# Plain float32 expert weights by DMA, and a waited memset behind every scatter: a four-layer kernel on one Trainium2 core

## The chip, the core and the metric

The kernel runs on one core of a Trainium2 chip. A core has five engines that run their own instruction streams and meet at semaphores: TensorE (PE, with its weight loads shown as PEld), VectorE (DVE), ScalarE (ACT), GpSimd (POOL) and SyncE (SP, which here only issues DMAs). Data come from HBM into SBUF by DMA; matmuls write PSUM. The metric is the device time of one execution in microseconds (us).

## What is computed

Eight sequences of 1024 tokens with 128 features go through four layers, each added to its input after a layer norm: linear attention, a mixture of experts, an RWKV-like mixing layer, and the same mixture of experts again. Cut to the part that the change touches:

```python
scores = x @ Wr.T + br                      # 8192 tokens, 8 experts
w = softmax(scores); idx = top_k(scores + biases, 2)
val = w[idx] / sum(w[idx])
h = x @ Wl1[e] + bl1[e]                     # 128 -> 2 x 256, only for the two chosen experts
y = (silu(h[:256]) * h[256:]) @ Wl2[e] + bl2[e]
out = sum over the two experts of val * y
```

## The kernel before, in words

**Stages.** Attention runs batch by batch (8 batches, each in two halves of 512 tokens) and ends each batch with the router: `choose` finds the two experts of each token, `place` ranks the tokens by expert and writes `place_i`, the queue row of each (line 1177). Then GpSimd scatters the batch's normalised tokens into `queue_dram`, sorted by expert (`scatter`, line 508): 16 indirect DMAs a batch, each of 128 rows. When all eight are queued, the first expert stage runs over 72 tiles of 256 queued tokens. The mixing layer then runs batch by batch, with router and scatter again, and the second expert stage follows.

**A tile of an expert stage.** SP loads 256 queued rows into `xtile` (lines 399 and 400). PE transposes them (955), ACT and DVE split the transposed tile into two float32r parts `xt_parts` (696, 1248). ACT copies the high part of the expert's up weights from SBUF into `tile_up` (700), DVE the low part (1253). PE makes three float32r matmuls for each of four 128-column chunks (946 to 948), ACT applies silu (690), DVE gates (1239), PE makes the down projection in float32 (965), DVE adds the bias into `ytile` (1259), and GpSimd scatters the two halves of `ytile` to `result_dram` (519). Loops hold eight tiles. The low part of all weights, `up_lo`, is made once in each expert stage by one DVE subtraction over 128 x 4096 elements (1223), in the plan that precedes the tiles.

**GpSimd's queue** sets much of the order. In attention its scatters of the batches 1 to 5 are paced: `pace` makes it wait for an event of PE between pairs of scatters. The batches 6 to 8, and all scatters of the mixing stage and of the expert stages, go back to back. In the mixing loop one turn of GpSimd's stream is `next_sums` (lines 553 and 555: four additions that make the layer's input two batches ahead), and then the 16 scatters of this batch. In `mixing`, DVE's stream has `way_in_moments` for the batch two ahead, which waits for those sums (`xsum_ready`), just before `choose` and `place`. The buffer `hffn[0]`, out of which a scatter reads, is single in the mixing layer: ACT (597) may write it for batch m only when the same half's scatters of batch m - 1 have landed (`queued`). In attention two buffers alternate.

## Time and profile before

| | us |
|---|---|
| median of three runs | 1330.14 |
| lowest, highest | 1322.95, 1336.12 |
| the profiled execution's own time | 1346.64 |
| its span, first to last instruction | 1344.8 |

| engine | busy us | share of the span |
|---|---|---|
| PE | 855.2 | 64% |
| DVE | 918.4 | 68% |
| ACT | 659.9 | 49% |
| POOL | 623.3 | 46% |

No engine is busy throughout, so the reader has to go stage by stage. Attention takes roughly the first 335 us of the span, the first expert stage 373 to 640, mixing 700 to 1000, the second expert stage 1040 to 1303. The profiled execution is 16.5 us slower than the median of the others; differences worked out on it are added to the median.

### The profile page before, as it was taken

How to read it: one execution, taken by the hardware profiler on the slowest of the kernel's cores; microseconds unless marked ns; L12 is line 12 of the kernel's file. 1: busy time of each engine (PE TensorE's matmuls, PEld its weight loads, DVE VectorE, ACT ScalarE, POOL GpSimd, SP SyncE). 2: the span in 40 equal slices, each digit the busy share in tenths (PEclk: the TensorE clock that was granted, in tenths of full speed). 3: DMA queues.
4: the chain of work that ended last, by engine and by line, in shares of the span. 5: the costliest groups of instructions: out<-in, count | busy, mean ns of one | idle time of the engine just before them, and what ended most of it. 6: DMA issues, size and time to landing. Idle time of an engine off the chain costs nothing.

```text
span 1344.8 us, 21163 instructions
## 1 busy us (share of the span) xinstructions
PE 855.2 (64%) x5110; PEld 697.5 (52%) x5111; DVE 918.4 (68%) x2976; ACT 659.9 (49%) x1788; POOL 623.3 (46%) x597
## 2 busy tenths in 40 slices
PE   3777777742178887776457667657423777887850
PEld 1665566542177887765123333323223777876750
DVE  5688888645465655555299999999953565655657
ACT  3676666611154444444576766655322444444435
POOL 3024444433545554545215555675434555555440
PEclk9788877856599888899677787787655899889885
DMA  7022222212222222221311222211092222222239
GB/s 223 16 60 79 78 79 80 65 53 68 83 75 74 68 76 69 71 58 49 110 60 63 69 83 86 94 47 38 30 254 66 71 69 75 73 70 69 62 97 315
DMA packets 144880, 111.79 MB, mean 83 GB/s; under 512 B 15779, under 2 KB 135724, under 8 KB 144464
## 3 DMA queue, kind: packets, MB, share of 16 engines
q1 hardware_dynamic: 126928, 77.58, 20.6%
q0 software_dynamic: 17920, 33.88, 7.9%
q8 instruction: 9, 0.15, 0.0%
q14 instruction: 23, 0.19, 0.0%
HBM read 62.84 MB, written 50.64 MB: 84 GB/s over the span
## 4 chain that ended last, share of the span: by engine, by line
DVE 31%; PE 31%; issue 13%; ACT 7%; another core or an unknown queue 5%; POOL 5%; DMA 4%; DVEq 2%; ACTq 1%; SPq 0%; POOLq 0%
PE banks L965 8%; PE banks L946 5%; POOL queue_dram L508 4%; PE banks L948 4%; PE banks L947 4%; DVE rope_c L1414 3%; PE banks L828 2%; PE banks L854 2%; DVE stats L1095 2%; PE banks L955 2%; ACT gated L690 1%; DVE gated L1239 1%; DMA out<-xmid 1%; DVE tile_up L1253 1%
## 5 line engine op out<-in xcount | busy, mean ns | idle before, releaser
L519 POOL DMA_INDIRECT result_dram<-ytile,result_row x288 | 283.9, 986 | 274.3 <-DVE ytile L1259 191.8
L508 POOL DMA_INDIRECT queue_dram<-hffn,place_i x192 | 222.9, 1161 | 205.8 <-DVE place_i L1177 120.6
L946 PE MATMUL banks<-xt_parts,tile_up 128*128 128x256 f32 x584 | 185.8, 318 | 87.4 <-DVE tile_up L1253 81.6
L1239 DVE SCALAR_TENSOR_TENSOR gated<-banks,tile_bias,gated 128x256 f32<-128x256 f32 x292 | 127.8, 479 | 99.9 <-ACT gated L690 76.4
L965 PE MATMUL banks<-wdown_sb,gated 128*128 x1152 | 171.2, 297 | 20.6 <-DVE gated L1239 20.5
L947 PE MATMUL banks<-xt_parts,tile_up 128*128 128x256 f32 x584 | 172.9, 296 | 0.0
L948 PE MATMUL banks<-xt_parts,tile_up 128*128 128x256 f32 x584 | 172.7, 296 | 0.0
L946 PEld LDWEIGHTS banks<-xt_parts,tile_up 128*128 128x128 f32 x584 | 119.9, 205 | 100.7 <-DVE xt_parts L1248 61.9
L965 PEld LDWEIGHTS banks<-wdown_sb,gated 128*128 128x128 f32 x1152 | 157.8, 211 | 24.3 <-issue 24.2
L690 ACT ACTIVATE gated<-banks,tile_bias 128x256 f32<-128x256 f32 x292 | 121.9, 470 | 97.4 <-PE banks L948 70.2
L696 ACT ACTIVATE xt_parts<-banks 128x256 fp32r<-128x256 f32 x150 | 57.8, 386 | 215.2 <-PE banks L955 171.7
L508 POOL DMA_INDIRECT queue_dram<-xtiles,place_i x64 | 62.3, 974 | 130.0 <-DVE place_i L1177 95.5
L947 PEld LDWEIGHTS banks<-xt_parts,tile_up 128*128 128x128 f32 x584 | 120.7, 207 | 0.0
L948 PEld LDWEIGHTS banks<-xt_parts,tile_up 128*128 128x128 f32 x584 | 120.3, 206 | 0.0
L1259 DVE TENSOR_TENSOR ytile<-banks,down_bias_sb 128x256 f32<-128x256 f32 x144 | 60.3, 419 | 86.8 <-PE banks L965 58.6
L700 ACT ACTIVATE tile_up<-up_hi 128x512 fp32r x148 | 93.3, 631 | 27.8 <-issue 27.8
L955 PE MATMUL banks<-k_sb,xtiles 128*128 128x128 f32 x300 | 62.8, 294 | 64.8 <-DMA xtiles<-queue_dram 64.8
L1248 DVE TENSOR_TENSOR xt_parts<-banks,xt_parts 128x256 fp32r<-128x256 f32 x150 | 62.8, 419 | 41.6 <-ACT xt_parts L696 33.9
L828 PE MATMUL banks<-k_sb,hmix 128*128 128x128 f32 x128 | 29.0, 370 | 86.1 <-ACT hmix L597 54.5
L955 PEld LDWEIGHTS banks<-k_sb,xtiles 128*128 128x128 f32 x300 | 41.4, 154 | 65.7 <-issue 64.0
L993 PE MATMUL banks<-hseq,wnow_sb 128*128 128x512 f32 x96 | 69.6, 815 | 6.2 <-ACT hseq L754 6.2
L828 PEld LDWEIGHTS banks<-k_sb,hmix 128*128 128x128 f32 x128 | 19.0, 185 | 98.8 <-ACT hmix L597 72.6
(210 smaller groups left out, 1986.8 us busy)
## 6 DMA issues: line engine op xcount, KB each, us to landing
xtiles<-queue_dram SPq DMA_DIRECT2D x160, 130.0 KB
qkv<-result_dram SPq DMA_DIRECT2D x24, 512.0 KB, 4.3
x_dram<-xres SPq DMA_DIRECT2D x32, 256.0 KB
result_dram<-ytile,result_row POOLq DMA_INDIRECT x288
xin<-x SPq DMA_DIRECT2D x16, 256.0 KB
xold<-x SPq DMA_DIRECT2D x16, 256.0 KB
expo<-w_up SPq DMA_DIRECT2D x2, 2048.0 KB, 9.3
xin<-x_dram SPq DMA_DIRECT2D x16, 256.0 KB
```

The source lines that it names most:

```text
L508: nc.gpsimd.indirect_dma_start(queue_dram, bass.IndirectOffsetOnAxis(ap=place_i[s][:, at:at + 1], axis=0), hffn[s][c][:, j, :], None).then ...
L519: nc.gpsimd.indirect_dma_start(result_dram, bass.IndirectOffsetOnAxis(ap=result_row[i][:, h:h + 1], axis=0), ytile[i][:, h, :], None, boun ...
L690: last = nc.scalar.activation(gated[at][:, h, :], ps_up[at][:, h, :], ACT.Silu, bias=tile_bias[(i + 1) % STEP][:, h:h + 1])
L700: nc.scalar.activation(tile_up[i % 2][:, 0, :], up_hi[:, bass.ds(e * (2 * HID), 2 * HID)].bitcast(F32), ACT.Copy).then_inc(whi_ready, 1)
L828: last = nc.tensor.transpose(dst[:, j * P:(j + 1) * P], src[:, j, 0:D], ident)
L946: nc.tensor.matmul(ps_up[at][:, h, :], hi, xt_parts[at][:, 0, :], start=True, stop=False)
L947: nc.tensor.matmul(ps_up[at][:, h, :], hi, xt_parts[at][:, 1, :], start=False, stop=False)
L948: last = nc.tensor.matmul(ps_up[at][:, h, :], lo, xt_parts[at][:, 0, :], start=False, stop=True)
L955: last = nc.tensor.transpose(ps_xt[(i + 3) % 2][:, part * P:(part + 1) * P], xtile[slot][:, part, 0:D], ident)
L965: last = nc.tensor.matmul(y, gated[i % 2][:, h, tokens], wdown_sb[:, bass.ds(e * (HCH * D) + h * D, D)], start=(h == 0), stop=(h == HCH - 1))
L993: nc.tensor.matmul(part, wnow_sb[:, i, :], hseq[:, 1 + c * CHUNK:1 + (c + 1) * CHUNK], start=True, stop=False)
L1239: last = nc.vector.scalar_tensor_tensor(gated[at][:, h, :], ps_up[at][:, HCH + h, :], tile_bias[(i + 1) % STEP][:, HCH + h:HCH + h + 1], g ...
```

## The change

Two things are changed at once.

**The expert stages.** The up projection is done in plain float32, with four matmuls a tile in place of twelve. The split of the tile (DVE 1248) and both weight copies (ACT 700, DVE 1253) go; ACT issues a 256 KB DMA a tile that brings the expert's up weights from HBM into one of four slots. ACT empties the transposed tile with one copy. `up_hi`, `up_lo` and their making (POOL 539, DVE 1223) go. Loops hold 12 tiles, `xtile` and `ytile` have 6 slots instead of 8, `gated` has 3 instead of 2, and PE works two tiles ahead of the down projection.

**The scatters.** Behind each of the 256 scatters to `queue_dram` and the 288 to `result_dram`, GpSimd clears a 128 x 16 buffer, waits for that memset's own semaphore, and clears the semaphore. The pacing by PE's events goes. `hffn` has two buffers of its own rather than sharing `xtiles`.

```diff
-STEP = 8
+STEP = 12
+SLOTS = 6
+WSLOTS = 4
+GSLOTS = 3
+SPACER = 16
@@ GpSimd
+            def space():
+                nc.gpsimd.memset(spacer[:], 0.0).then_inc(spaced, 1)
+                pool.wait_ge(spaced, 1)
+                pool.sem_clear(spaced)
...
-            def scatter(m, s, paced):
+            def scatter(m, s):
...
-                        if paced and c + j:
-                            pace(m, c * TPC + j)
-                            pool.sem_inc(place_taken, 1)
                         for k in range(TOPK):
...
                                 hffn[s][c][:, j, :], None).then_inc(queued[s][c], 16)
+                            space()
...
+                                ytile[i % SLOTS][:, h, :], None, bounds_check=NO_RESULT - 1, oob_is_err=False).then_inc(y_stored[i % SLOTS], 16)
+                            space()
...
-            pool.wait_ge(experts_in, 16 * len(EXPERTS))
-            nc.gpsimd.tensor_copy(up_hi[:], up_raw).then_inc(hi_ready, 1)
@@ ACT
-                    nc.scalar.activation(xt_parts[(i + 3) % 2][:, 0, :], ps_xt[(i + 3) % 2], ACT.Copy).then_inc(xhi_ready, 1)
+                    nc.scalar.activation(xt[i % 2][:], ps_xt[i % 2], ACT.Copy).then_inc(xt_ready, 1)
...
-                    nc.scalar.activation(tile_up[i % 2][:, 0, :], up_hi[:, bass.ds(e * (2 * HID), 2 * HID)].bitcast(F32), ACT.Copy).then_inc(whi_ready, 1)
+                    nc.scalar.dma_start(tile_up[i % WSLOTS][:], w_up[:, bass.ds(e * (2 * HID), 2 * HID)]).then_inc(tile_up_in[i % WSLOTS], 16)
@@ PE
-                        nc.tensor.matmul(ps_up[at][:, h, :], hi, xt_parts[at][:, 0, :], start=True, stop=False)
-                        nc.tensor.matmul(ps_up[at][:, h, :], hi, xt_parts[at][:, 1, :], start=False, stop=False)
-                        last = nc.tensor.matmul(ps_up[at][:, h, :], lo, xt_parts[at][:, 0, :], start=False, stop=True)
+                        last = nc.tensor.matmul(ps_up[i % 2][:, h, :], tile_up[i % WSLOTS][:, h * P:(h + 1) * P], xt[i % 2][:],
+                                                start=True, stop=True)
@@ DVE
-                nc.vector.tensor_tensor(up_lo[:], up_raw, up_hi[:].bitcast(F32), ALU.subtract).then_inc(lo_ready, 1)
...
-                    nc.vector.tensor_tensor(xt_parts[at][:, 1, :], ps_xt[at], xt_parts[at][:, 0, :].bitcast(F32),
-                                            ALU.subtract).then_inc(xlo_ready, 1)
...
-                    nc.vector.tensor_copy(tile_up[i % 2][:, 1, :], up_lo[:, bass.ds(e * (2 * HID), 2 * HID)].bitcast(F32)).then_inc(wlo_ready, 1)
```

On GpSimd, at the start of an expert stage, the stores of the first two tiles and a half stood like this before (519 is the scatter of one half of `ytile`, the register row belongs to the loop):

```order
L514 UNCONDITIONAL_BRANCH
L514 ISA
L519 DMA result_dram<-ytile,result_row 16520x128 [waits ytile_ready]
L519 DMA result_dram<-ytile,result_row 16520x128
L516 REGISTER_ALU
L519 DMA result_dram<-ytile,result_row 16520x128 [waits ytile_ready]
L519 DMA result_dram<-ytile,result_row 16520x128
```

The same place of the changed kernel (515 is now that scatter, 491 the memset, 493 the clear of its semaphore, which carries the wait):

```order
L515 DMA result_dram<-ytile,result_row 16518x128 [waits ytile_ready]
L491 MEMSET spacer 128x16
L493 ISA [waits spaced]
L515 DMA result_dram<-ytile,result_row 16518x128
L491 MEMSET spacer 128x16
L493 ISA [waits spaced]
L512 REGISTER_ALU
L515 DMA result_dram<-ytile,result_row 16518x128 [waits ytile_ready]
```

Between any two scatters there now stand a memset and a wait for it. The scatters to `queue_dram` (503 now) have the same three rows each.

On DVE, one tile of the expert loop before:

```order
L1231 SCALAR_TENSOR_TENSOR result_row<-xtiles,expert_all 128x2
L1253 ISA
L1253 COPY tile_up<-up_lo 128x512
L1239 SCALAR_TENSOR_TENSOR gated<-banks,tile_bias,gated 128x256 [waits silu_ready]
L1239 SCALAR_TENSOR_TENSOR gated<-banks,tile_bias,gated 128x256
L1259 ISA [waits y_stored1,y_ready]
L1259 TENSOR_TENSOR ytile<-banks,down_bias_sb 128x256
L1245 ISA
L1245 COPY tile_bias<-up_bias_sb 128x4
L1246 REGISTER_ALU
L1248 TENSOR_TENSOR xt_parts<-banks,xt_parts 128x256 [waits xhi_ready]
```

and one tile of it now (1243 gates, 1251 adds the bias, 1232 makes the result rows, 1237 takes the bias columns):

```order
L1243 SCALAR_TENSOR_TENSOR gated<-banks,tile_bias,gated 128x256 [waits silu_ready]
L1243 SCALAR_TENSOR_TENSOR gated<-banks,tile_bias,gated 128x256
L1249 REGISTER_ALU
L1251 ISA [waits y_stored1,y_ready]
L1251 TENSOR_TENSOR ytile<-banks,down_bias_sb 128x256
L1232 ISA [waits y_stored4,xtile_in4]
L1232 SCALAR_TENSOR_TENSOR result_row<-xtile,expert_all 128x2
L1237 ISA
L1237 COPY tile_bias<-up_bias_sb 128x4
```

The weight copy and the split are gone, and the bias addition stands directly behind the gate of the tile two ahead.

## Rows read from the trace of the kernel before

**Rows 1.** The page's head: the profiled span.

```profile
span 1344.8 us, 21163 instructions
```

**Rows 2.** Timeline, expert stage: start us, us, engine, line, operation [idle before <-releaser].

```profile
401.05 0.42 DVE L1259 TENSOR_TENSOR ytile<-banks,down_bias_sb 128x256 f32<-128x256 f32 x1 [1.63 <-remote]
...
402.35 0.98 POOL L519 DMA_INDIRECT result_dram<-ytile,result_row  x1 [2.31 <-DVE ytile L1259]
...
403.97 1.06 PE L965 MATMUL banks<-wdown_sb,gated 128*128 x8
...
404.87 0.38 PE L955 MATMUL banks<-k_sb,xtiles 128*128 128x128 f32 x2
...
408.18 0.38 ACT L696 ACTIVATE xt_parts<-banks 128x256 fp32r<-128x256 f32 x1 [2.98 <-PE banks L955]
```

**Rows 3.** Scatters to results: duration ns min/median/max, first and last start us.

```profile
L519 POOL DMA_INDIRECT result_dram<-ytile,result_row x288: 980/983/1182, 373.5 to 1301.8; - x144
```

**Rows 4.** Timeline, POOL: last result scatter of stage one, first of two.

```profile
637.27 0.98 POOL L519 DMA_INDIRECT result_dram<-ytile,result_row  x1 [0.30 <-issue]
...
1040.05 1.00 POOL L519 DMA_INDIRECT result_dram<-ytile,result_row  x1 [15.57 <-DVE ytile L1259]
```

**Rows 5.** Windows, one mixing batch: busy us (x) of PE, PEld, DVE, ACT, POOL; PEclk, DMA, GB/s.

```profile
755.47:796.13 40.66, 27.82 (x85) 15.15 (x85) 38.93 (x100) 25.88 (x53) 24.88 (x20) 0.75 0.25 78
```

**Rows 6.** Timeline of that mixing batch, POOL and DVE.

```profile
756.30 2.66 POOL L508 DMA_INDIRECT queue_dram<-hffn,place_i  x1 [11.04 <-DVE place_i L1177]
...
779.44 0.96 POOL L508 DMA_INDIRECT queue_dram<-hffn,place_i  x1 [0.30 <-issue]
780.43 1.27 POOL L553 TENSOR_TENSOR xold<-xin,qkv 128x512 f32<-128x512 f32 x1
...
784.34 1.60 POOL L555 TENSOR_TENSOR xold<-xold,qkv 128x512 f32<-128x512 f32 x1
...
787.87 1.65 DVE L1095 BATCH_NORM_STATS2 stats<-xold 128x6 f32<-128x128 f32 x8 [0.19 <-DVE rotated L1380]
...
795.96 0.17 DVE L1177 CAST place_i<-place_f 128x16 int32<-128x16 f32 x1
...
796.95 2.67 POOL L508 DMA_INDIRECT queue_dram<-hffn,place_i  x1 [11.01 <-DVE place_i L1177]
```

**Rows 7.** Timeline, POOL: a memset at the kernel's start.

```profile
0.22 0.10 POOL L1572 MEMSET const-float32-0.0<- 128x1 f32 x1 [0.22 <-issue]
```

**Rows 8.** Timeline: last scatter of batch 15 of 16, and who waits for it.

```profile
980.13 0.96 POOL L508 DMA_INDIRECT queue_dram<-hffn,place_i  x1 [0.30 <-issue]
...
986.19 0.17 DVE L1146 COPY hffn<-k_sb 128x4 f32<-128x4 f32 x1 [5.12 <-DMA queue_dram<-hffn,place_i]
```

**Rows 9.** Timeline, POOL: first scatters of the attention batches 5, 6 and 7.

```profile
223.66 0.96 POOL L508 DMA_INDIRECT queue_dram<-xtiles,place_i  x1 [7.62 <-DVE place_i L1177]
...
257.64 0.96 POOL L508 DMA_INDIRECT queue_dram<-hffn,place_i  x1 [7.64 <-DVE place_i L1177]
...
297.64 0.96 POOL L508 DMA_INDIRECT queue_dram<-xtiles,place_i  x1 [19.93 <-DVE place_i L1177]
```

**Rows 10.** Timeline, POOL: first, eighth and last scatter of batch 16.

```profile
998.30 0.95 POOL L508 DMA_INDIRECT queue_dram<-hffn,place_i  x1 [17.21 <-DVE place_i L1177]
...
1009.20 5.19 POOL L508 DMA_INDIRECT queue_dram<-hffn,place_i  x1 [0.31 <-issue]
...
1023.52 0.96 POOL L508 DMA_INDIRECT queue_dram<-hffn,place_i  x1 [0.31 <-issue]
```

**Rows 11.** DVE's work on `up_lo`: duration ns min/median/max, first and last start us.

```profile
L1253 DVE CAST tile_up<-up_lo x148: 414/421/657, 364.4 to 1297.6; 128x512 fp32r x148
L1223 DVE TENSOR_TENSOR up_lo<-expo,up_hi x2: 4418/4418/4419, 343.0 to 1009.1; 128x4096 fp32r<-128x4096 f32 x2
```

**Rows 12.** Timeline, PE: one float32 matmul with 512 columns, as two instructions.

```profile
794.92 1.02 PE L994 MATMUL banks<-hseq,wpast_sb 128*128 128x512 f32 x2
```

**Rows 13.** DMA issues: count, KB, median us to landing.

```profile
expo<-w_up SPq DMA_DIRECT2D x2, 2048.0 KB, 9.3
```

More of the change, by code:

```diff
@@ L144, in program @@
             rotated = [rotated0, rotated1]
[L145 removed]
+        tile_up = [sb(f"tile_up{i}", [P, 2 * HID]) for i in range(WSLOTS)]
         rope2 = sb("rope2", [P, TPC, 2 * D])
@@ L321, in program @@
         FIRST, SECOND = 0, 1
-        N_TURN, N_WEIGHTS, N_UP, N_GATE, N_BACK = (XTILES + ahead for ahead in (3, 2, 1, 1, 0))
         PLACE_STEPS = 3
@@ new lines, in weights, with steps @@
+                def weights(i, e):
+                    nc.scalar.dma_start(tile_up[i % WSLOTS][:], w_up[:, bass.ds(e * (2 * HID), 2 * HID)]).then_inc(tile_up_in[i % WSLOTS], 16)
+                def steps(n, left):
+                    first = n * STEP
+                    e = read(mybir.EngineType.Activation, tile_expert[0:1, bass.ds(first + 2 + WSLOTS, min(STEP, left - 2 - WSLOTS))], NE - 1)
+                    for i in range(STEP):
+                        if i + 2 < left:
+                            silu_up(first + i + 2, i + 2)
+                        if i + 2 + WSLOTS < left:
+                            weights(i + 2 + WSLOTS, e[i])
+                        if i + 4 < left:
+                            empty_x(first + i + 4, i + 4)
@@ new lines, in experts @@
+                act.wait_ge(table_ready, f + 1)
+                e = read(mybir.EngineType.Activation, tile_expert[0:1, 0:2 + WSLOTS], NE - 1)
+                for t in range(WSLOTS):
+                    weights(t, e[t])
+                empty_x(0, 0)
+                empty_x(1, 1)
+                for t in range(2):
+                    silu_up(t, t)
+                    weights(t + WSLOTS, e[t + WSLOTS])
+                    empty_x(t + 2, t + 2)
+                with act.Fori(0, LAST) as n:
+                    steps(n, 2 * STEP)
@@ L720, in weigh @@
+                steps(LAST, STEP)
             def weigh(y, g, done, first=0, step=1):
@@ L964, in down, with steps @@
                         for h in range(HCH):
-                            last = nc.tensor.matmul(y, gated[i % 2][:, h, tokens], wdown_sb[:, bass.ds(e * (HCH * D) + h * D, D)],
+                            last = nc.tensor.matmul(y, gated[i % GSLOTS][:, h, tokens], wdown_sb[:, bass.ds(e * (HCH * D) + h * D, D)],
                                                     start=(h == 0), stop=(h == HCH - 1))
                     last.then_inc(y_ready, 1)
-                pe.wait_ge(table_ready, f + 1)
-                for t in range(-3, 0):
-                    if t + 1 >= 0:
-                        up(t, t)
-                    turn_x(t, t)
-                with pe.Fori(0, XTILES // STEP) as n:
-                    first = n * STEP
-                    e = read(mybir.EngineType.PE, tile_expert[0:1, bass.ds(first, STEP)], NE - 1)
-                    for i in range(STEP):
-                        up(first + i, i)
-                        down(first + i, i, e[i])
-                        turn_x(first + i, i)
+                def steps(n, left):
+                    e = read(mybir.EngineType.PE, tile_expert[0:1, bass.ds(n * STEP, STEP)], NE - 1)
+                    for i in range(STEP):
+                        if i + 2 < left:
+                            up(n, i + 2)
+                        if i + 4 < left:
+                            turn_x(n, i + 4)
+                        down(n, i, e[i])
+                pe.wait_ge(table_ready, f + 1)
+                turn_x(0, 0)
+                turn_x(0, 1)
+                for t in range(2):
+                    up(0, t)
+                    turn_x(0, t + 2)
+                with pe.Fori(0, LAST) as n:
+                    steps(n, 2 * STEP)
+                steps(LAST, STEP)
             def turn_in(m):
@@ new lines, in steps @@
+                def steps(n, left):
+                    e = read(mybir.EngineType.DVE, tile_expert[0:1, bass.ds(n * STEP, min(STEP + 4, left))], NE - 1)
+                    for i in range(STEP):
+                        if i + 2 < left:
+                            gate(n, i + 2)
+                        add_bias(n, i, e[i])
+                        if i + 3 < left:
+                            place_rows(n, i + 3)
+                        if i + 4 < left:
+                            take_bias(i + 4, e[i + 4])
@@ L1282, in invert_norms @@
+                dve.wait_ge(table_ready, f + 1)
+                e = read(mybir.EngineType.DVE, tile_expert[0:1, 0:4], NE - 1)
+                for t in range(4):
+                    take_bias(t, e[t])
+                for t in range(3):
+                    place_rows(0, t)
+                for t in range(2):
+                    gate(0, t)
+                with dve.Fori(0, LAST) as n:
+                    steps(n, 2 * STEP)
+                steps(LAST, STEP)
             def invert_norms(m):
```

221 lines of the change are left out of this document (81 added, 140 removed).

## The prediction, made before the changed kernel ran

> **What bounds the kernel now.** I read the windows by stage first, then the timeline of one expert tile and of one mixing batch, because the shares of the whole span say nothing (no engine is over 70%).
>
> In the expert stages GpSimd makes 144 result scatters each. The first starts at 373.5 and the last at 637.27, and in the second stage they run from 1040.05 to 1301.8 [rows 3, 4]: 143 steps of 1.845 and of 1.83 us, or 3.69 us a tile. A scatter takes 0.98 us, and one without a wait before it starts 0.30 after the last, a step of 1.28 [rows 4], so GpSimd alone would need 2.6 us a tile. It idles because its input is late, and the timeline shows why: PE's transposes of a tile are shown as done at 405.25, and ACT, which waits for nothing else, copies them at 408.18, 2.9 us late [rows 2], while scatters run back to back. So PE's messages get through late during bursts of scatters, and this costs the stage about 1 us a tile. I take that as the thing that a pause behind each scatter can cure.
>
> In mixing a batch takes 40.66 us, and DVE is busy for 38.93 of them [rows 5]. But GpSimd is nearly as tight. Its chain: 16 scatters from 756.30, the last starting at 779.44; sums from 780.43 to 785.94; DVE takes the sums at 787.87 and ends `place` at 796.13; the next scatter starts at 796.95 [rows 6]. The sums are ready only 1.93 us before DVE wants them. This is a closed loop (scatters, sums, moments, place, scatters) with 1.93 us of slack in 40.65.
>
> **The price of a paused scatter.** This is the term on which all rests. A scatter that follows a wait starts late: `ytile` is ready at 401.47 and the scatter starts at 402.35, 0.88 later [rows 2]; `place_i` is ready at 796.13 and the scatter starts at 796.95, 0.82 later [rows 6]. Without a wait the gap is 0.30 [rows 4], since the next scatter is made ready while the last runs. The new wait takes that overlap away. Between the end of a scatter and the next start there then are: 0.03 to the memset (a POOL addition starts 0.03 after a scatter's end [rows 6]), 0.10 for the memset [rows 7] (1 column there, 16 here; I take 0.11), 0.05 for the clear (no POOL row; between nothing and the wait's own 0.1), and 0.82 or 0.88. For `queue_dram` a step becomes 0.96 + 0.03 + 0.11 + 0.05 + 0.82 = **1.97 us** against 1.26; for the results 0.98 + 0.03 + 0.11 + 0.05 + 0.88 = **2.05**, I use 2.04. Bounds: the cheapest is that the wait costs only the memset, 1.26 + 0.14 = 1.40; the dearest that DVE keeps the memsets waiting too, 2.2.
>
> **Expert stages.** Is another engine over the 2 x 2.04 = 4.08 us that GpSimd now needs for a tile? PE: a float32 matmul of 512 columns is two instructions that end within 1.02 us, so 0.43 each once they follow one another (1.02 less the last one's 0.59), thus 0.21 for 256 columns; eight of them make 1.7 for up. Down takes 0.9 (eight instructions from 403.97 to the transposes at 404.87) and the transposes 0.25 [rows 2, 12]. That is 2.85 a tile, less than 4.08. DVE loses a weight copy of 0.42 [rows 11] and the split, ACT a copy, and none of this lies on GpSimd's path any more. The weight DMA carries 256 KB; 2048 KB landed in 9.3 us [rows 13], so one lands between 1.2 and 9.3, and it is issued four tiles, 16 us, ahead: hidden. ACT's issue of it is hidden by ACT's idle time, since only one copy and two activations a tile are left to it. With six slots GpSimd finds finished tiles waiting, so what PE and DVE save is not seen. Each stage: 143 x (2.04 - 1.845) = **+27.9**, and 143 x (2.04 - 1.83) = **+30.0**. The cure of PE's late messages is real and is worth nothing here, because the new bound is above the old.
>
> **Mixing.** The 16 scatters spanned 23.14 us between first and last start, where 15 x 1.26 = 18.9: 4.2 us are lost to DVE (one scatter took 2.66 [rows 6]). I keep the 4.2. New: 15 x 1.97 + 4.2 = 33.7 to the last start, 1.2 to its end, memset and sums' start, 5.5 of sums (780.43 to 785.94), 0.1, then 8.26 of DVE from the moments to `place` (787.87 to 796.13), and 0.82: 49.6 against 40.65, +8.9 a batch. This holds for the five intervals inside the loop: +45. For the last two batches the sums are not in the way but the buffer is: in batch 15 the last scatter starts at 980.13 and DVE and ACT may write at 986.19, 6.1 later; the next scatter starts at 998.30, 12.1 after that [rows 8, 10]. With a landing of 4 us (6.1 in a burst is the upper bound) the interval is 33.7 + 4 + 12.1 = 49.8 against 41.3 now: +8 each, +16. Together **+61**.
>
> **Scatters that nothing hides.** After batch 16 all wait for its scatters: 998.30 to 1023.52, 25.22 us [rows 10]. Of these 4.2 are the scatter at 1009.20, held for 5.19 us while DVE makes `up_lo` for 4.42 [rows 10, 11]; that goes. New: 15 x 1.97 + 2.05 of other stalls = 31.6, **+6.4**. After batch 8 it is the same, +6.4. Against it stands attention: batch 6 takes 33.98 from batch 5 (paced), batch 7 takes 40.0 behind unpaced scatters [rows 9]; the pause gives back these 6.0. GpSimd needs 0.8 + 16 x 1.97 = 32.3 us a batch, just under the 33.98, so attention is not stretched. Net **+0.4**.
>
> Here a rule of the Trainium skill bears on the sum. The rows show that DVE's 148 weight copies of 0.42 us leave the result scatters alone, at 980, 983 and at most 1182 ns [rows 3, 11], while the subtraction into `up_lo` holds a scatter for 5.19 us [rows 10]. The page "SBUF — State Buffer", section "SBUF: two separate sides", says that a DVE copy in float32 within SBUF locks GpSimd out of its port, so that it can't write descriptors. By that rule the change would also free up to 148 x 0.42 = 62 us by dropping the copies (an estimate by that page); by the row it frees only the subtraction. The row decides.
>
> **Sum.** 27.9 + 30.0 + 61 + 6.4 + 0.4 = 125.7. The span of 1344.8 [rows 1] becomes 1471, the profiled execution's 1346.6 becomes 1472, and the median of 1330.1 becomes 1456. I say 1455.
>
> **Rivals.**
> (1) *The pause is cheap, and the expert stages run at PE's pace* (ends on the other side). If a pause costs only the memset, steps are 1.40, GpSimd needs 2.8 a tile and PE's 2.85 decides, some 3.1 with the granted clock below full now and then. A stage of 72 tiles is 223 us against 264, twice -41; mixing +3; attention -6; the bare scatters -4. About 1240. For: late messages of PE are in the trace. Against: 0.82 and 0.88 stand before every scatter with a wait. It decides below a step of about 1.68: the sum falls by 4.2 us for each 0.01 of the step (286 steps in the experts, 105 in mixing, 30 bare).
> (2) *Mixing is not stretched.* DVE at 38.93 of 40.66 looks like the bound, and if sums or buffers have slack that I don't see, the 61 fall away: 1395. Against: 1.93 us between sums and moments.
> (3) *The pause is dearer.* If DVE's long operations hold memsets as they hold scatters, a step is 2.2: +0.2 x 421 = +84, so 1540. To this belongs the clock: mixing is granted 0.75 [rows 5]; with PE idle for a third of each tile, the expert stages may fall to the lower of its two levels. At 0.75 a tile is 2.85 / 0.75 = 3.8, still under 4.08; at the lower level throughout it is 5.7, +117 a stage. The Trainium skill, page "TensorE: Matmul & The Clock Gate", section "HAM oscillation — how this bites in real kernels", says that idle gaps of PE bring the clock down; by it this would come true wherever PE waits for GpSimd, but a PE at half clock would be busy again, so I give it little.
>
> **How the numbers follow.** Forecast (1400 to 1505): 0.63. Rival 1: 0.12. Rival 2: 0.12. Rival 3: 0.13. The range reaches down to rival 2 and up to where the step is 2.15, and leaves out rival 1 and the end of rival 3: 1380 to 1530. About 1% is what a measurement can tell from no change. Faster by over 1% is rival 1, 0.12; within 1% needs the step between 1.65 and 1.71, 0.02; slower 0.86.
>
> **What would show it.** Right: result scatters about 2.04 apart without idle time by `ytile`, windows of a mixing batch near 49.6, ACT's copy of a transposed tile directly after PE. Wrong: GpSimd idle for `ytile` in the expert stages (then PE or ACT's DMA issue is the bound), steps of 1.4 to 1.7 between scatters, or DVE without a wait for the sums in mixing.

## The result, and the profile after

The changed kernel takes 1488.40 us (median of four, 1485.62 to 1491.13) against 1333.13 for the kernel before on the same chip (median of four, 1322.95 to 1338.26): 1.1175 times as long, 95% interval 1.1102 to 1.1249. Slower, as forecast, and inside the range of 1380 to 1530, 33 us above the predicted 1455. The profiled execution took 1485.62 us; its span is 1483.4 against 1344.8 [rows 1], so +138.6 on the spans where the sum said +125.7. Of all the executions reported below one, of `e4_late_wait`, ran at a mean granted clock of 0.67 (0.77 to 0.81 in the others) and took 1331.54 us; it is left out of the figures of that kernel.

The page of the changed kernel, its head and the groups that carry the change (the columns are: count | busy us, mean ns of one | idle us of the engine before them, and what ended most of it):

```profile
span 1483.4 us, 20450 instructions
...
PE 893.9 (60%) x4498; PEld 695.6 (47%) x4499; DVE 780.1 (53%) x2662; ACT 574.5 (39%) x1630; POOL 691.4 (47%) x1138
...
L503 POOL DMA_INDIRECT queue_dram<-hffn,place_i x256 | 290.1, 1133 | 368.2 <-POOL spacer L491 171.3
L515 POOL DMA_INDIRECT result_dram<-ytile,result_row x288 | 282.8, 982 | 314.7 <-POOL spacer L491 135.4
...
L491 POOL MEMSET spacer<- 128x16 f32 x544 | 75.8, 139 | 0.3
```

The scatters last as long as before (982 ns, [rows 3]), yet GpSimd now idles 683 us before them (368.2 and 314.7), and the largest single part of each is put down to its own clear (171.3 and 135.4). The shares of PE, DVE and ACT fell (64, 68 and 49% before). The timeline of POOL in the expert stage shows one pause after the other:

```profile
450.77 0.98 POOL L515 DMA_INDIRECT result_dram<-ytile,result_row  x1 [0.86 <-issue]
451.74 0.14 POOL L491 MEMSET spacer<- 128x16 f32 x1
452.90 0.98 POOL L515 DMA_INDIRECT result_dram<-ytile,result_row  x1 [1.02 <-POOL spacer L491]
453.86 0.14 POOL L491 MEMSET spacer<- 128x16 f32 x1
454.87 0.98 POOL L515 DMA_INDIRECT result_dram<-ytile,result_row  x1 [0.86 <-issue]
```

From one scatter to the next it is 2.13 and 1.97 us in turn, where rows 4 show 1.28 without a wait. The clear itself takes 0.14; the 0.86 and 1.02 behind it are GpSimd with nothing to do until its next scatter begins. The longer one stands ahead of a tile's first scatter, behind the wait for `ytile`, the loop's sum and a semaphore count.

The waits of the first expert stage, 375 to 668 us (engine, line, what it waited for: us in total, times, longest):

```profile
DVE result_row L1232 <- DMA result_dram<-ytile,result_row: 163.7, 63, 5.1
...
POOL result_dram L515 <- issue: 67.3, 68, 3.4
POOL result_dram L515 <- POOL spacer L491: 63.9, 66, 1.0
...
POOL result_dram L515 <- DVE ytile L1251: 7.1, 7, 1.0
```

GpSimd waits for a finished tile 7 times, 7.1 us in all, and each of these waits is as long as the 1.02 us that stand there anyway. VectorE stands 163.7 us until a scatter out of the slot that it wants has landed, and ACT and TensorE wait behind VectorE.

And one mixing batch, its window from one end of `place` to the next (columns as in rows 5), with POOL's and VectorE's places in it:

```profile
845.17:894.50 49.33, 28.00 (x87) 14.67 (x85) 36.23 (x100) 26.44 (x53) 27.03 (x36) 0.72 0.21 64
```

```profile
846.00 2.65 POOL L503 DMA_INDIRECT queue_dram<-hffn,place_i  x1 [9.19 <-DVE place_i L1184]
...
878.98 0.96 POOL L503 DMA_INDIRECT queue_dram<-hffn,place_i  x1 [0.80 <-POOL spacer L491]
...
880.97 1.25 POOL L544 TENSOR_TENSOR xold<-xin,qkv 128x512 f32<-128x512 f32 x1 [0.89 <-POOL spacer L491]
...
884.87 1.26 POOL L546 TENSOR_TENSOR xold<-xold,qkv 128x512 f32<-128x512 f32 x1
...
886.24 1.65 DVE L1102 BATCH_NORM_STATS2 stats<-xold 128x6 f32<-128x128 f32 x8 [11.98 <-POOL xold L546]
...
894.32 0.17 DVE L1184 CAST place_i<-place_f 128x16 int32<-128x16 f32 x1
...
895.32 2.65 POOL L503 DMA_INDIRECT queue_dram<-hffn,place_i  x1 [9.18 <-DVE place_i L1184]
```

VectorE, busy for 38.93 of 40.66 us before [rows 5], now stands some 12 us in each batch (11.98 in this one) waiting for GpSimd's sums. It no longer bounds the batch.

Stage by stage, from the starts of scatters and the ends of `place`:

| stretch | before | after | difference | forecast |
|---|---|---|---|---|
| start to `place` of batch 1 | 89.7 | 89.0 | -0.7 | |
| to `place` of batch 8 | 241.8 | 220.3 | -21.4 | |
| to the last scatter of batch 8 | 25.9 | 42.7 | +16.7 | these three +0.4 |
| to the first result scatter | 16.2 | 18.6 | +2.4 | 0 |
| first to last result scatter | 263.8 | 298.6 | +34.9 | +27.9 |
| to `place` of batch 9 | 77.4 | 77.3 | 0.0 | 0 |
| to `place` of batch 14 | 203.5 | 247.6 | +44.1 | +45 |
| to `place` of batch 16 | 79.3 | 97.6 | +18.3 | +16 |
| to the last scatter of batch 16 | 26.1 | 32.0 | +6.0 | +6.4 |
| to the first result scatter | 16.5 | 18.8 | +2.2 | 0 |
| first to last result scatter | 261.7 | 298.0 | +36.3 | +30.0 |
| to the end | 43.0 | 42.9 | -0.1 | 0 |

### The profile page after: what moved, and what is told of

It reads as the page before. It is cut to its first block, busy times and chain, and to the rows that moved or that the text cites. A ratio compares the mean times of both kernels' runs of the same rounds, so it can differ in the third digit from the quotient of the medians.

```text
span 1483.4 us, 20450 instructions
## 1 busy us (share of the span) xinstructions
PE 893.9 (60%) x4498; PEld 695.6 (47%) x4499; DVE 780.1 (53%) x2662; ACT 574.5 (39%) x1630; POOL 691.4 (47%) x1138
## 4 chain that ended last, share of the span: by engine, by line
POOL 42%; issue 32%; DVE 8%; DMA 6%; PE 6%; ACT 3%; POOLq 2%; DVEq 1%; SPq 0%; ACTq 0%
POOL queue_dram L503 19%; POOL result_dram L515 16%; POOL spacer L491 6%; DMA result_dram<-ytile,result_row 2%; PE banks L854 1%; DMA out<-xmid 1%; PE banks L945 1%; POOL xold L544 1%; POOLq L493 1%; DVE stats L1102 1%; DMA queue_dram<-hffn,place_i 1%; PE banks L882 1%; DVE gated L1243 1%; PE banks L828 1%; DVE top_at L1162 1%
## 5 line engine op out<-in xcount | busy, mean ns | idle before, releaser
L503 POOL DMA_INDIRECT queue_dram<-hffn,place_i x256 | 290.1, 1133 | 368.2 <-POOL spacer L491 171.3
L515 POOL DMA_INDIRECT result_dram<-ytile,result_row x288 | 282.8, 982 | 314.7 <-POOL spacer L491 135.4
L945 PE MATMUL banks<-xt,tile_up 128*128 128x256 f32 x1152 | 292.7, 399 | 119.6 <-DVE gated L1243 119.5
L945 PEld LDWEIGHTS banks<-xt,tile_up 128*128 128x128 f32 x1152 | 215.0, 197 | 161.3 <-issue 118.7
L1232 DVE SCALAR_TENSOR_TENSOR result_row<-xtile,expert_all 128x2 int32<-128x2 f32 x144 | 31.9, 221 | 394.4 <-DMA result_dram<-ytile,result_row 326.3
L953 PE MATMUL banks<-k_sb,xtile 128*128 128x128 f32 x288 | 58.1, 285 | 87.5 <-DMA xtile<-queue_dram 87.5
L953 PEld LDWEIGHTS banks<-k_sb,xtile 128*128 128x128 f32 x288 | 42.1, 148 | 104.0 <-issue 88.4
L687 ACT ACTIVATE xt<-banks 128x256 f32<-128x256 f32 x144 | 55.3, 384 | 73.3 <-PE banks L953 73.3
L491 POOL MEMSET spacer<- 128x16 f32 x544 | 75.8, 139 | 0.3
L723 ACT ACTIVATE qkv<-qkv,gate 128x128 f32<-128x128 f32 x160 | 48.5, 388 | 68.0 <-DMA qkv<-result_dram 67.3
L854 PE MATMUL banks<-wqkv_sb,hmix_t 128*128 128x384 f32 x128 | 60.0, 554 | 9.4 <-DMA bias_rows<-split_dram 7.7
L1001 PE MATMUL banks<-hseq,wpast_sb 128*128 128x512 f32 x96 | 64.3, 760 | 0.0
```

The lines of the kernel that those rows point to most:

```text
L491: nc.gpsimd.memset(spacer[:], 0.0).then_inc(spaced, 1)
L503: nc.gpsimd.indirect_dma_start(queue_dram, bass.IndirectOffsetOnAxis(ap=place_i[s][:, at:at + 1], axis=0), hffn[s][c][:, j, :], None).then ...
L515: nc.gpsimd.indirect_dma_start(result_dram, bass.IndirectOffsetOnAxis(ap=result_row[i % SLOTS][:, h:h + 1], axis=0), ytile[i % SLOTS][:, h ...
L854: nc.tensor.matmul(dst, hmix_t[c][:, j * P:(j + 1) * P], wqkv_sb[:], start=True, stop=False)
L945: last = nc.tensor.matmul(ps_up[i % 2][:, h, :], tile_up[i % WSLOTS][:, h * P:(h + 1) * P], xt[i % 2][:], start=True, stop=True)
L953: last = nc.tensor.transpose(ps_xt[i % 2][:, part * P:(part + 1) * P], xtile[i % SLOTS][:, part, 0:D], ident)
```

## The experiments

Every run was measured beside the kernel before on its own chip, and the first thing that they showed was about that kernel. Three chips run the kernel before in 1179 to 1181 us, not in 1333. The last run came to a chip where it takes 1333 again (it may be the chip of the first comparison). I call them quick and slow chips.

### The pause alone, and the rest alone

`e1_pause_only` puts the pause into the kernel before and takes the pacing waits out; its expert stages stay as they were. `e2_no_pause` is the changed kernel without the pause.

```diff
# e1_pause_only, against before, behind every scatter
+                            space()
# and scatter(..., False) everywhere
```

```diff
# e2_no_pause, against after, at both places
-                            space()
```

> The kernel before with the memset and its wait behind every scatter and without pacing; the expert stages stay as they were (float32r in three products, weight copies in SBUF). Theory A (GpSimd's step alone sets the expert and the mixing stages): steps of 1.90 us for queue scatters and 2.05 for result scatters, an expert tile every 4.1 us, a mixing batch every 49.3 us, 1480 to 1500 us in all. Rival B (the new expert stages, with float32 and weight DMAs, carry the loss): expert tiles at 3.7 us or less, a total near 1400.

> The changed kernel with the memset, its wait and its clear taken out, so scatters go back to back everywhere and unpaced; the expert stages are the new ones. Theory A (the pause is the loss, and PE's messages are late during bursts of scatters whatever the matmuls are): mixing batch back at 40.7 us, expert tile 3.6 to 3.9 us because of late messages, attention batches near 40 us; 1340 to 1375 us. Rival B (the new expert stages are themselves slow): more than 1400. Rival C (late messages belong to the float32r stage alone): expert tile near 3.0, total near 1280.

Measured: `e1_pause_only` 1493.05 us (1490.18 to 1495.66) beside 1181.16, ratio 1.264 (1.2611 to 1.2668), as expected. `e2_no_pause` 1196.74 (1193.41 to 1198.17), ratio 1.0138 (1.0121 to 1.0156). All three totals that I had given for `e2_no_pause` were too high (1280 at the least): they were worked out from the trace of the slow chip. The pause is nearly the whole of the change. What is left, the new expert stages without their pause and without the pacing, costs 1.4% there. Without the pause TensorE is the bound of those stages. This is its window in `e2_no_pause`, columns as in rows 5:

```profile
350.00:540.00 190.00, 190.00 (x1206) 173.14 (x1205) 99.15 (x334) 74.17 (x201) 131.49 (x134) 1.00 0.60 177
```

It is busy for all 190.00 us at a granted clock of 1.00, the higher level (2.4 GHz). The stage takes 201.9 us from first to last result scatter, 2.82 a tile, where the forecast's own estimate of TensorE's work was 2.85. So rival 1's picture of the bound was right and only its premise, a cheap pause, was not.

### The two places of the pause

`e3_pause_stores` keeps it behind the result scatters only, `e8_pause_scatters` behind the queue scatters only.

```diff
# e3_pause_stores, against after, in scatter()
-                            space()
```

```diff
# e8_pause_scatters, against after, in experts()
-                            space()
```

> The changed kernel with the pause behind the result scatters alone; queue scatters go back to back and unpaced. Theory A (closed loop of scatters, sums, moments and place in mixing): mixing batch 40.7 us again, bare scatters 6 us shorter each, attention batches up to 40 us instead of 32; expert tile unchanged at 4.09. 1415 to 1450 us. Rival B (mixing is stretched by something other than the queue scatters' step): mixing stays near 49 us, total near 1490.

> The changed kernel with the pause behind the queue scatters alone, the other half of the run that had it behind the result scatters alone (1391.5 us against 1196.7 without any). If the pauses of the two places add up (each stage bound in its own place), it takes 1196.7 + 1488.4 - 1391.5 = 1294 us (1285 to 1302): mixing batches 49.4 us, attention batch 8 and batch 16 bare scatters at 1.90 us, expert stages 202 us. If they share a part (a stage start that either of them delays), 1270 to 1285 us.

Measured: 1391.53 us and 1291.81 (1290.88 to 1295.56). Over `e2_no_pause` that is +194.8 and +95.1, together 289.9; the whole pause costs 1486.2 - 1196.7 = 289.5 on a quick chip. The halves add up, so each stage is bound in its own place. In the trace of `e3_pause_stores` the expert stages take 298.6 and 298.9 us and everything else is as in `e2_no_pause` within 1.5 us; in `e8_pause_scatters` the expert stages take 201.6 each, five mixing batches 247.0 against 203.3, and batch 16's scatters 32.0. I had put `e3_pause_stores` at 1415 to 1450, too high, because that was worked out from the trace of the slow chip.

### The wait, not the clear

`e4_late_wait` keeps all three instructions in another order: behind a scatter it waits for the clear that was made ahead of that scatter, and only then makes the next one, so the wait finds its semaphore already there.

```diff
 def space():
-    nc.gpsimd.memset(spacer[:], 0.0).then_inc(spaced, 1)
     pool.wait_ge(spaced, 1)
     pool.sem_clear(spaced)
+    nc.gpsimd.memset(spacer[:], 0.0).then_inc(spaced, 1)
# and one memset ahead of the first scatter
```

> The changed kernel with the same three instructions behind each scatter in another order: the wait and the clear for the previous memset come first, then this one's memset, so that the wait never holds GpSimd. Theory A (the price of the pause is the lost overlap of making the next scatter ready, 0.5 us, not the memset): steps of 1.40 to 1.45 us, mixing batch 41 to 43 us. What the expert tile does tells whether the idle time or the memset cures the late messages: with the cure 3.0 to 3.2 us and a total near 1270; without it 3.7 and a total near 1370. Rival B (memset and clear are the price): steps stay near 1.9 and 2.05, total near 1485.

Measured: 1199.33 us (median of three, 1192.86 to 1202.51), ratio to before 1.0142 (1.0091 to 1.0194), 3 above `e2_no_pause`, with a mixing batch of 40.7 us and expert stages of 201.1 and 201.0. Its POOL timeline:

```profile
320.14 0.96 POOL L503 DMA_INDIRECT queue_dram<-hffn,place_i  x1 [0.18 <-POOL spacer L493]
321.11 0.12 POOL L493 MEMSET spacer<- 128x16 f32 x1
321.41 0.96 POOL L503 DMA_INDIRECT queue_dram<-hffn,place_i  x1 [0.18 <-POOL spacer L493]
```

A step is 1.27 us, the same as with no clear at all (1.26): the 0.12 of the clear lies in the 0.30 that stood between two scatters anyway. I had said 1.40 to 1.45, because I added the clear to the step. So 544 clears cost next to nothing, and 544 waits that hold the queue cost 287 us (1486.2 less 1199.3). Whether the clears or the idle time cure late messages, as I had asked, this run can't tell, since its chip had none. I read this so: the next scatter is made ready while the last one runs, and only a wait that is still open takes that away. The Trainium skill, page "Perfetto Trace Analysis", section "DMA Instruction — SWDGE (GPSIMD)", names the steps between a met wait and the descriptors (from a wait queue to a FIFO, then to the DSPs) but gives them no times. The rows here give 0.81 to 1.02 us from the end of the clear to the next scatter, for all of them with the clear of the semaphore.

### How the time follows the length of the pause

```diff
-SPACER = 16
+SPACER = 256
```

> The changed kernel with 256 scratch columns cleared in place of 16, so that each pause is longer by d us (d read from the clear's own rows; 0.1 to 0.4). Theory A (the pause is on the closed path of GpSimd in every expert tile and every mixing batch): each expert stage longer by 143 x d, each of the eight mixing batches by 16 x d, the bare scatters of batch 8 and 16 by 15 x d each: about 286 + 128 + 30 = 444 us for each us of d, so 1486 + 44 = 1530 us for d = 0.1, 1575 for 0.2. Attention batches 1 to 7 stand at 31.5 us against 16 x 1.90 = 30.4 us of scatters, and join in once d is over 0.07, which adds up to 112 x (d - 0.07). Rival (the mixing batches are closed by the landing of the last scatter and only half of the scatters lie in it): 8 x d for each mixing batch, 380 us for each us of d.

Measured: 1585.99 us (1584.14 to 1589.60) against 1486.2 for the changed kernel on a quick chip. The clears' own row gives d:

```profile
L491 POOL MEMSET spacer<- x544: 325/340/429, 90.5 to 1540.7; 128x256 f32 x182
```

340 ns in place of 141, d = 0.20 us. The expert stages are longer by 28.7 and 28.6 us, and 143 x 0.20 is 28.6. A mixing batch is longer by 1.93, which is neither 16 x d (3.2) nor 8 x d (1.6). All 16 steps are in the loop, but beside VectorE's work some scatters last up to 2.65 us, and the later they come, the fewer they meet: from the first scatter of a batch to the sums it is 36.9 us against 35.0, so the clears' 3.2 come out as 1.9. The stretch from the first `place` to batch 8's last scatter is longer by 24.0, nearly 120 x d. GpSimd was on the path there from the first batch on, not from d = 0.07, as I had it. In all 5.0 us for each 0.01 of the step, where the forecast said 4.2 and what I expected of this run, with attention joined in, comes to 5.2 at most for this d.

### Why the kernel before is 154 us apart on two chips

> The kernel before, unchanged, to have its trace on a chip where its median was 1181.16 us and not 1333.13. Theory A (late matmul reports): in the trace of before at 1344.8 us, 259 semaphore updates of TensorE in the expert stages come over 0.3 us late (up to some 3 us) while GpSimd issues result scatters one behind the other, and an expert stage takes 263.8 us from its first result scatter to its last. At 1181 us they come within 0.01 us, an expert stage takes 195 to 203 us (2.72 to 2.82 us a tile, TensorE's own pace at the full clock), attention batches 1 to 8 216 us in place of 241.8, and mixing stays at 40.65 us a batch. Theory B (clock): the granted clock is higher all through and every matmul shorter, mixing too: mixing batches of 37 us or less, expert tiles no nearer to TensorE's busy time than before.

> The changed kernel, unchanged, beside the kernel before on whatever chip this is. If the chip moves only the kernel before (theory A: GpSimd's paced pause bounds the changed kernel, and TensorE's reports have slack there), 1483 to 1495 us whatever before takes, so that the ratio is 1.25 to 1.27 where before is at 1181 and 1.11 to 1.13 where it is at 1333. If the chip moves both alike (theory B), 1310 to 1340 us beside 1181.

Measured, both kernels unchanged: 1178.90 us (1177.07 to 1184.55) and 1486.20 (1483.02 to 1488.75), ratio of the second to before 1.2593 (1.255 to 1.2636). The changed kernel takes the same on both chips (1488.4 and 1486.2), the kernel before doesn't. The new kernel's time came as expected; for the expert stage of the kernel before I had said 195 to 203 us. The stages of the two traces of before:

| stretch | slow chip | quick chip |
|---|---|---|
| `place` of batch 1 to batch 8 | 241.8 | 216.9 |
| first expert stage | 263.8 | 191.3 |
| `place` of batch 9 to 14 | 203.5 | 203.3 |
| second expert stage | 261.7 | 191.2 |

Mixing is the same, so it is no matter of the clock as a whole. The granted clock is 0.74 in mixing on both; in the first expert stage it is 0.92 on the slow chip and 1.00 on the quick one, too little for 263.8 us against 191.3. The expert stages and attention differ, and the waits of the first expert stage say in what. First the slow chip (380 to 635 us), then the quick one (352 to 539):

```profile
POOL result_dram L519 <- DVE ytile L1259: 79.2, 32, 3.8
ACT xt_parts L696 <- PE banks L955: 64.3, 30, 3.6
...
PE banks L946 <- DVE tile_up L1253: 38.1, 24, 3.6
DVE gated L1239 <- ACT gated L690: 37.0, 46, 3.8
```

```profile
DVE gated L1239 <- ACT gated L690: 29.1, 62, 0.7
...
POOL result_dram L519 <- DVE ytile L1259: 20.9, 53, 1.1
ACT xt_parts L696 <- PE banks L955: 17.5, 62, 0.5
...
PE banks L946 <- DVE tile_up L1253: 6.2, 8, 0.9
```

ACT waits for TensorE's transposes 2.1 us at a time (up to 3.6) on the one and 0.28 (at most 0.5) on the other. Where ACT had been idle before, its copy starts 0.04 us after the end of the transposes in every one of 62 tiles on the quick chip. On the slow one the median is 0.39 and the longest 2.91. VectorE too starts late behind TensorE on the slow chip, its bias addition 0.7 us behind the down projection in the median. What VectorE and TensorE wait for from others comes in time there: where VectorE waits with a gate, it starts 0.03 us behind ACT's silu on both chips, and TensorE's first up matmul 0.15 behind VectorE's weight copy. So it is TensorE's messages that are late. (The trace of the slow chip also holds fewer semaphore events for the same program, 11,068 against 17,490, so I go by the starts of instructions and not by the recorded events.)

In attention few messages are late, but some of them by much. In batch 7 of the slow chip, while the unpaced scatters of batch 6 run, ACT stands still for 7.89 us before it squares the second half of an output whose last matmul TensorE had ended at 265.17 (ACT's rows, then TensorE's last row before that wait ends):

```profile
266.57 0.30 ACT L629 ACTIVATE out_dev<-out_sum,rms_eps 128x4 f32<-128x4 f32 x1
274.76 0.28 ACT L626 ACTIVATE out_squares<-banks 128x128 f32<-128x128 f32 x1 [7.89 <-remote]
```

```profile
265.95 0.60 PE L828 MATMUL banks<-k_sb,qf 128*128 128x128 f32 x4
```

On the quick chip ACT does the same two things with no time between them (258.52 and 258.73). Ends of matmuls are modelled in a profile, but TensorE has nothing else to do in those 8 us, so a matmul that ended later than shown doesn't explain them. Scatters that run back to back are not enough to make messages late, though: in mixing on the slow chip ACT and VectorE waited 20 times for an end of TensorE that fell among such scatters, and only 2 of these waits ended over 0.3 us late, none over 0.8.

Do bursts of scatters make them late? A kernel with a pause only behind every second scatter tells, if it comes to a slow chip.

```diff
# e7, e11 and e12, against before
# scatter(), batches 1 to 7 (and 6 and 7 paced as well)
-                            pace(m, c * TPC + j)
-                            pool.sem_inc(place_taken, 1)
+                            space()
# experts(), behind the two scatters of a tile
+                        space()
```

> The kernel before with the waited clear behind every pair of scatters in attention batches 1 to 7 (in place of the waits that pace them) and behind the second of the two result scatters of each tile; none in the mixing batches. A tile then costs GpSimd 1.29 + 1.97 to 2.13 = 3.3 to 3.4 us. If late reports of TensorE come from scatters one behind the other, this kernel is free of them on every chip: 71.5 steps of 3.35 = 240 us a stage, so about 1181 + 2 x 42 = 1265 us where before takes 1181, and still about 1265 us where before takes 1333, faster than it. If the late reports belong to the execution and not to the bursts, it takes 1265 us where before takes 1181 and 1330 us or more where before takes 1333.

> The kernel before with a pause behind every second scatter, once more, for the case that this chip runs the kernel before at some 1330 us: then it tells whether the late reports of the engines come from bursts of scatters (1297 us, faster than before) or from the chip (1330 us or more). Where before takes 1179 us it should repeat 1297 us and tells nothing new.

> The kernel before with a pause behind every second scatter, a third time, for the same question: where this chip runs the kernel before at some 1330 us, 1297 us says that bursts of scatters make the reports of the engines late, 1330 us or more that they are late on that chip whatever GpSimd does. Where before takes 1179 us it repeats 1297 to 1299 us and the question stays open.

On the quick chips: 1297.52 us (1295.87 to 1300.25), ratio 1.0986 (1.0953 to 1.1019), and 1299.41. I had said 1265. The stage starts from 191.3 us, not 198, and a tile costs GpSimd 1.29 + 2.13 = 3.42 in the median, not 3.35, and 3.5 in the mean with the turns of the loop. Its timeline:

```profile
450.73 0.15 POOL L502 MEMSET spacer<- 128x16 f32 x1
451.90 1.02 POOL L527 DMA_INDIRECT result_dram<-ytile,result_row  x1 [1.02 <-POOL spacer L502]
453.23 0.98 POOL L527 DMA_INDIRECT result_dram<-ytile,result_row  x1 [0.30 <-issue]
454.19 0.15 POOL L502 MEMSET spacer<- 128x16 f32 x1
455.36 1.02 POOL L527 DMA_INDIRECT result_dram<-ytile,result_row  x1 [1.02 <-POOL spacer L502]
```

The third time it met a slow chip: 1297.58 us (1296.84 to 1298.32) where before takes 1332.61, ratio 0.971 (0.9595 to 0.9824). Its expert stages take 249.6 us there and 249.9 on the quick chip. So one and the same kernel is 3% faster than before on the one chip (2 to 4% by the interval) and 10% slower on the other. The waits of ACT in its first expert stage on the slow chip, then on the quick one:

```profile
ACT gated L699 <- PE banks L957: 53.9, 40, 4.5
...
ACT xt_parts L705 <- PE banks L964: 12.7, 30, 1.3
```

```profile
ACT gated L699 <- PE banks L957: 76.7, 62, 4.5
ACT xt_parts L705 <- PE banks L964: 17.1, 62, 0.5
```

The longest wait for the transposes is 1.3 us, not 3.6. Some lateness is left (ACT's copy up to 1.00 us behind the transposes, 0.04 in the median), and GpSimd's pauses cover it. This agrees with the forecast's reading that messages are late while scatters run close together, and that a pause thins it. It doesn't tell the two effects of a pause apart, messages in time and a bound that no longer feels them. Why one chip has this and the other not stays open, and so does why mixing hardly feels it.

### One instruction moved, and faster than both

```diff
# e10_low_early, against before
             attention(None, 1, 2)
+            dve.wait_ge(hi_ready, 1)
+            nc.vector.tensor_tensor(up_lo[:], up_raw, up_hi[:].bitcast(F32), ALU.subtract).then_inc(lo_ready, 1)
# and the same instruction left out of plan(FIRST)
```

> The kernel before with one instruction moved: VectorE's 4.42 us subtraction that makes up_lo for the first expert stage runs behind attention batch 0, not in the plan behind batch 8, where a queue scatter of GpSimd lasts 5.19 us beside it in every trace of before (0.96 otherwise). If the subtraction holds the scatter, the last scatter of batch 8 comes 3.3 to 4.3 us earlier after the last place of the stage, and 1179 becomes 1175 us (0.3 per cent), with one scatter of 5.19 us or none left in the whole trace. If the long scatter has another cause, it stays where it is and the time too, 1179 us.

Measured over five rounds: 1173.80 us (1170.26 to 1176.05) against 1178.91, ratio 0.9953 (0.9936 to 0.997), 5.1 us less and clear of the noise. Three scatters of batch 8, and the moved subtraction:

```profile
317.80 1.01 POOL L508 DMA_INDIRECT queue_dram<-hffn,place_i  x1 [0.30 <-issue]
319.12 0.95 POOL L508 DMA_INDIRECT queue_dram<-hffn,place_i  x1 [0.30 <-issue]
320.37 0.96 POOL L508 DMA_INDIRECT queue_dram<-hffn,place_i  x1 [0.30 <-issue]
```

```profile
L1479 DVE TENSOR_TENSOR up_lo<-expo,up_hi x1: 4425/4425/4425, 52.4 to 52.4; 128x4096 fp32r<-128x4096 f32 x1
```

No scatter of batch 8 is held any more, its last one starts 21.7 us after `place` in place of 25.9, and the one of 5.19 us in batch 16, beside the subtraction that stayed [rows 10], is still there. So VectorE's long subtraction of two operands in SBUF does hold a scatter, shown by moving it. At 52.4 us no scatter runs yet. Whether it costs anything there can't be said: from the start to `place` of batch 8 this trace takes 308.7 us against 306.9, but two traces of the kernel with pairs differ by 2.5 between `place` of batch 1 and of batch 8 (218.7 and 216.2).

## Why the prediction was right, step by step

**The pause: right, both terms a little off.** A step of queue scatters was put at 1.97 and is 1.90: the clear is 0.125 (0.11 said), and from its end to the next scatter it is 0.81, with the semaphore's clear inside it and not 0.05 beside it. A step of result scatters was put at 2.04 and is 1.97 and 2.13 in turn, 2.05. A wait that is still open costs what stood before every waiting scatter in rows 2 and 6, and `e4_late_wait` shows that it is the wait.

**Expert stages: the mechanism right, the size 7 and 6 us short.** The tile was put at 4.08 us and takes 4.18 in the mean. The steady tile is 4.10; the rest are steps that are longer than usual, one of 2.5 us at the turn of each round of 12 tiles, four of 2.3 and one of 4.5. The 7 waits for `ytile` add nothing. That GpSimd and not TensorE (2.85 a tile) would be the bound held: `ytile` is waited for 7.1 us in all. That the new expert code is worth nothing under the pause held nearly: with the old code `e1_pause_only` takes 7 us more. Of the signs that the forecast named, the steps, the mixing window and VectorE's wait for the sums came as said. ACT's copy directly behind the transposes can't be read off: in the steady part of the stages ACT never stands idle before it.

**Stage starts: left out.** From the last scatter of a batch to the first result scatter it is 2.4 and 2.2 us more. `e2_no_pause` has it too (+1.8 and +3.0 against before on a quick chip), so it comes with the new expert code and not with the pause. The sum had no term for it.

**Mixing: right in place, and in size with some luck.** 62.4 us against 61. The loop's parts were 33.7 + 1.2 + 5.5 + 0.1 + 8.26 + 0.82 and are 33.0 to the last scatter's start, 2.0 to the sums, 5.2 of sums, 0.1, 8.3 and 0.8: 49.3 against the 49.6 of the forecast. The 1.2 left out the wait ahead of the sums (0.89 behind the clear), which the shorter step gave back. The last two intervals are 47.8 and 49.8 us, where 49.8 was said for both, and before they were 37.5 and 41.8, where 41.3 was said for both. The two errors nearly cancel: +18.3 against +16, where 49.8 twice less the true 79.3 would have been +20.3.

**Scatters that nothing hides.** +6.0 against +6.4 after batch 16. After batch 8 it was +16.7, not +6.4: GpSimd enters batch 8 behind, its first scatter 11.7 us after `place` in place of 1.0.

**Attention: the step that failed.** The text said that the pause gives back only the 6.0 of batch 7, because 32.3 us of GpSimd fit into a batch of 33.98. But 33.98 was itself stretched: the same interval is 31.05 on a quick chip, and batches 1 to 8 take 241.8 us on this chip and 216.9 on a quick one. The forecast saw late messages in the expert stages, where ACT copied 2.9 us late [rows 2], and did not look for them in attention, where the wait of 7.89 us stood in its own trace. The new kernel's batches come at nearly the quick pace, and GpSimd, which takes 31 to 34 us for each, falls behind: its first scatter comes 3.5 to 8 us after `place` in the batches 2 to 7. That is -21.4 up to `place` of batch 8 and +16.7 behind it. 7.9 and 7.9 of the 21.4 lie in the intervals of the batches 7 and 8, behind scatters that were not paced before either, so there it is the pause that gives them back (`e12_pairs_third`, on a slow chip too, has these intervals at 31.9 and 26.8, the new kernel at 32.1 and 26.7, the kernel before at 40.0 and 34.6); for the rest no run on a slow chip parts the pause from the pacing that went. From the start to the last scatter of batch 8 it nets -5.4 against +0.4.

**The medians: a step that failed by 16 us.** The sum was made on the profiled execution's span and its distance of 16.5 us to the median carried over to the new kernel. By four runs the old distance is 13.5 us, and the new kernel's profiled execution lies 2.8 below its median (1485.6 against 1488.4): together the 16. Where the old distance came from isn't shown. The kernel before ranges from 1323 to 1344 on slow chips, and its profiled execution, 1346.6, lies just outside; on the quick chips there is no such distance. The sum short by 13, this by 16, and a rounding by 1 and a later median of before by 3 make up the 33 us between 1455 and 1488. The 13 are themselves small by luck: the expert stages, their starts and mixing were short by 19, and attention gave 6 of them back.

**The rivals.** Rival 1 (a cheap pause) fell: a step of 1.68 was the limit and it is 1.90 and 2.05. Rival 2 (mixing not stretched) fell by the window of 49.33. Rival 3 fell too: VectorE's long operations hardly hold the clears (6 of 544 took over 200 ns, 537 at most), and the granted clock over the expert stage, from its window, is 0.93:

```profile
375.00:668.00 293.00, 213.56 (x1214) 186.15 (x1212) 97.46 (x337) 74.15 (x200) 155.71 (x281) 0.93 0.40 114
```

TensorE waits there for a quarter of the time and is at the higher level (2.4 GHz) for most of it all the same.

**What no step of it could say.** The 11.8% hold for a slow chip. On a quick one the same change costs 25.9%, because there the expert stages of the kernel before take 191.3 us and not 263.8: no late messages hide part of the pause. The forecast's sum on the trace of a quick chip would have had 143 x (2.04 - 1.34) = 100 us for each expert stage; it is 107.

## What to carry to other kernels

A wait that is still open between two indirect DMAs of GpSimd made each step longer here by 0.64 us for queue scatters and 0.76 for result scatters, though the work waited for took 0.13 to 0.14. If something must be waited for, wait for what was started one item earlier. Before a time is read as a property of a kernel, ask whether another chip gives it: this kernel, whose engines live closely on each other's messages, differed by 13% between chips, and the same kernel held back by GpSimd's pauses did not.

## What the runs showed of the hardware that I had not expected

- The same program takes 1179 to 1181 us on three chips and 1333 in two comparisons on chips of the other kind, with single runs within 1% of these. The difference lies in the expert stages and in attention, where ACT and VectorE start up to some 3 us and once 8 us late behind TensorE; mixing takes the same on both. Bound by GpSimd's pauses, the kernel takes 1486 and 1488.
- A clear of 128x16 between two scatters is free (step 1.27 us with it, 1.26 without) if nobody waits for it.
- From the end of the clear to a tile's first scatter it is 1.02 us and to its second 0.86. The difference shows in every tile.
- VectorE's subtraction of 4.42 us from SBUF to SBUF with two inputs holds a scatter for 5.19 us; the 148 copies of 0.42 us from SBUF to SBUF, which write float32r, leave them at 980 ns [rows 3, 11]. The Trainium skill, page "SBUF — State Buffer", section "SBUF: two separate sides", has a DVE copy in float32 lock GpSimd out, and an operation with two SBUF inputs only against a GpSimd operation that reads SBUF. The rows show it of the subtraction and not of the copies.
